# Third layer of a fused four-layer kernel: state scan and feed-forward in one phase instead of two, with a written-out order of their TensorE products

## The reference

```python
h = _layernorm(hidden_states, ln_w, ln_b)
z, x, Bm, Cm, dt = jnp.split(h @ in_proj_w.T, ...)       # widths 512, 128, 128, 512, 8
dt = softplus(dt + dt_bias); A = -exp(A_log)
# 8 heads of 64, state 64, 2 key groups:
#   state = state * exp(dt*A) + dt * x (outer) B ;  y = state . C
y = scan(x, dt, A, B, C) + Dp * x
yf = y * silu(z)
yf = yf * rsqrt(mean(yf * yf) + EPS) * norm_w
mlp = gelu(h @ fc1_w.T + fc1_b) @ fc2_w.T + fc2_b        # inner width 1024
return yf @ out_proj_w.T + mlp + residual
```

## Time and profile before

| | |
|---|---|
| median of 3 runs | 4635.87 us (4613.26 to 4637.77) |
| profiled execution | 4619.02 us, span 4617.3 us |
| third layer from the start of the scan phase to its last add | 1816.1 to 2315.4 us of the span |
| granted TensorE clock, mean of the span | 0.911 of 2.4 GHz |

### The profile page before, as it was taken

The page is one execution under the profiler, slowest core; times in us unless marked ns, Lnnn a source line. Parts: engine busy times, 40 slices in busy tenths (PEclk is TensorE's granted clock), DMA queues, the critical chain, the costliest instruction groups (busy, mean ns, idle before and its releaser), DMA issues. The chain is left out here.

```text
span 4617.3 us, 104974 instructions
## 1 busy us (share of the span) xinstructions
PE 3973.5 (86%) x45271; PEld 2429.6 (53%) x45330; DVE 2323.8 (50%) x4264; ACT 1675.7 (36%) x2628; POOL 1225.8 (27%) x1755
## 2 busy tenths in 40 slices
PE   7887759999975885877989958999999999999869
PEld 3333645555533653444745635666666666656636
DVE  5663244445553134244033245776767676766641
ACT  2345122121121111323111034666556655665532
POOL 2000110000014033131000015555545554555512
PEclk9999669999986986888989978999999999999979
DMA  1000000000012331000010000000000000000000
GB/s 49 1 1 1 29 25 1 11 11 1 11 48 77 122 112 44 0 0 23 0 56 0 0 14 7 10 9 9 9 9 9 11 11 10 9 9 9 7 15 19
DMA packets 38110, 92.10 MB, mean 20 GB/s; under 512 B 7136, under 2 KB 27267, under 8 KB 34142
## 3 DMA queue, kind: packets, MB, share of 16 engines
q1 hardware_dynamic: 27294, 69.66, 4.5%
q0 software_dynamic: 6144, 11.62, 0.9%
q10 hardware_dynamic: 4224, 4.19, 0.3%
HBM read 70.18 MB, written 20.45 MB: 20 GB/s over the span
## 5 line engine op out<-in xcount | busy, mean ns | idle before, releaser
L2622 PE MATMUL ps<-h_normT,h_w 128*128 128x512 f32 (+1 forms) x1008 | 423.6, 525 | 28.5 <-DVE h_xx L3209 20.9
L3143 DVE SCALAR_TENSOR_TENSOR h_cv<-h_raw,h_cw,h_cv 128x1023 f32<-128x1023 f32 (+2 forms) x288 | 391.0, 1367 | 20.2 <-ACT h_cv L2970 19.1
L3287 DVE SCALAR_TENSOR_TENSOR h_st<-h_st,d_gcs,ps 128x64 f32<-128x64 f32 x448 | 123.4, 275 | 341.2 <-PE ps L2918 340.9
L2969 ACT ACTIVATE h_raw<-ps 128x512 f32<-128x512 f32 x192 | 114.1, 594 | 399.1 <-PE ps L2622 398.4
L2622 PEld LDWEIGHTS ps<-h_normT,h_w 128*128 128x128 f32 x1008 | 164.7, 189 | 133.8 <-issue 116.6
L956 PE MATMUL ps<-a_probT,a_v 128*128 128x512 f32 x512 | 227.8, 604 | 0.9 <-DVE a_probT L1094 0.9
L472 ACT ACTIVATE a_prob<-ps 128x1024 f32<-128x1024 f32 (+1 forms) x192 | 154.4, 810 | 194.2 <-PE ps L384 104.3
L2519 POOL TENSOR_TENSOR h_gm<-h_gm,h_tmp 128x15 f32<-128x15 f32 (+7 forms) x480 | 214.9, 448 | 37.6
L2084 PE MATMUL ps<-h_normT,e_wgu 128*128 128x512 f32 (+1 forms) x448 | 204.3, 599 | 6.2 <-DMA e_wd<-in_e_wd 5.0
L1243 POOL MEMSET r_zero<- 128x2048 f32 x1 | 1.8, 1805 | 727.8 <-POOLq L54 727.8
L2918 PEld LDWEIGHTS ps<-h_st,h_mT 64*64 64x64 f32 x1792 | 90.5, 133 | 198.3 <-issue 194.2
(11 more groups left out here) (540 smaller groups left out, 9359.5 us busy)
## 6 DMA issues: line engine op xcount, KB each, us to landing
m_wgu<-in_m_wgu SPq DMA_DIRECT2D x8, 1408.0 KB
h_w<-in_d_w SPq DMA_DIRECT2D x48, 128.0 KB
m_wd<-in_m_wd SPq DMA_DIRECT2D x8, 704.0 KB
m_rows_in<-r_zero SPq DMA_DIRECT2D x4, 1024.0 KB
e_xe<-m_rows_in SPq DMA_DIRECT2D x8, 512.0 KB
m_rows_out<-e_y ACTq DMA_DIRECT2D x8, 512.0 KB
e_wgu<-in_e_wgu SPq DMA_DIRECT2D x1, 3520.0 KB
a_t_raw<-in_t_w SPq DMA_DIRECT2D x4, 768.0 KB
```

Of the source, the lines that this page charges most:

```text
L2622: last = pe.matmul(ps[:, PROJ[m], lo:hi], w[:, kind, k, :], hT[:, k, b * S + tb * BANK + lo:b * S + tb * BANK + hi], start=(k == 0), stop= ...
L3143: dve.scalar_tensor_tensor(out=d, in0=raw[:, kind, 0:S - back], scalar=tap(pr, kind, TAPS3 - 1 - back), in1=d, op0=ALU.mult, op1=ALU.add). ...
```

## The change

`scan2` and `mlp2` become one phase, `scan_mlp2`. All weights are loaded at its start. What it does to the work:

- The token products lose their one-row product; VectorE adds the `dt` bias as it evicts. The decay sums are put between the 10th and the 11th of the 20 B and C products.
- The decay and C-B products are done half by half (`seg(n, g)`, `cb(n, g)`), each half in one bank, and one round ahead of the tile that uses them. The exponential and the multiplication are halved too.
- Two banks form a ring that the inner-layer products (`up`), the gate (`z`) and the turning of y (`turn`) use by a fixed list (`entries`). An entry waits until the entry two before it has been evicted.
- The inner layer is formed for one tile of each sequence at a time (256 columns), two of its four quarters in each round. Its products, and those with `out_proj` and `fc2` (`outputs`), stand between the products of the scan.
- The scaling by the root moves behind the `out_proj` product: VectorE multiplies the product with it as it adds to the residual; `norm_w` is multiplied into `out_proj` once. The mean square and its root are taken tile by tile. GpSimd adds the `fc2` bias to the residual.

The diff, cut to its core:

```diff
 def mixer2(core):
 
 
-    nc = core.nc
-    with Phase(core, "s2") as outer:
-        y = outer.sb("y", [P, NT, DI2])
-        affine_norm2(core)
-        scan2(core, y)
-        mlp2(core, y)
+    affine_norm2(core)
+    scan_mlp2(core)
...
+        SEG, CB, RING, INTRA, INTER, UPD, OUT = 0, 1, (2, 3), 4, 5, 6, 7
...
+        entries = [("up", 0, q) for q in range(4)] + [("z", 0)]
+        for i in range(NT + 1):
+            if i >= 1:
+                entries.append(("turn", i - 1))
+            if i // 2 + 1 < NB:
+                entries += [("up", i // 2 + 1, 2 * (i % 2) + q) for q in range(2)]
+            if i + 1 < NT:
+                entries.append(("z", i + 1))
+        slot = {e: i for i, e in enumerate(entries)}
+        bank = lambda *e: RING[slot[e] % 2]
...
+            sp.dma_start(b2[:], dram["s2_b2"].broadcast_to([P, H])).then_inc(load_mlp, 16)
+            for dst, name in ((f1, "s2_f1"), (b1, "s2_b1"), (op, "s2_op"), (nw, "s2_nw"), (f2, "s2_f2")):
+                sp.dma_start(dst[:], dram[name]).then_inc(load_mlp, 16)
...
+            pool.wait_ge(load_mlp, 16 * 6)
+            for t in range(NT):
+                last = pool.tensor_tensor(core.x[:, t, :], core.x[:, t, :], b2[:], ALU.add)
+            last.then_inc(biased, 1)
...
-                pe.matmul(ps[:, t % 4, 0:TOKW2], core.ones[0:1, :], dtb[0:1, :], start=False, stop=True).then_inc(tokp, 1)
...
+            def room(*e):
+                if slot[e] >= 2:
+                    pe.wait_ge(evicted, slot[e] - 1)
+
+            def seg(n, g):
                 pe.wait_ge(seg_in, n + 1)
-                if n >= 1:
-                    pe.wait_ge(dec_e, n)
-                for g in range(KV2):
-                    pe.matmul(ps[:, g, :], after[:], dseg[:, s, g * J2:(g + 1) * J2, :].rearrange("p h t -> p (h t)"),
-                              start=True, stop=False)
-                    last = pe.matmul(ps[:, g, :], identb[:], notyet[:].rearrange("p h t -> p (h t)"), start=False, stop=True)
-                last.then_inc(segp, 1)
-                if n >= 1:
-                    pe.wait_ge(m_r, n)
-                for g in range(KV2):
-                    last = pe.matmul(ps[:, 2 + g, :], bT[:, g, cols], cT[:, :, cols], start=True, stop=True)
-                last.then_inc(cbp, 1)
-                if n >= 1:
-                    pe.wait_ge(z_r, n)
+                if 2 * n + g >= 1:
+                    pe.wait_ge(dec_e, 2 * n + g)
+                pe.matmul(ps[:, SEG, :], after[:], dseg[:, n % 2, grp(n, g), :].rearrange("p h t -> p (h t)"), start=True, stop=False)
+                pe.matmul(ps[:, SEG, :], identb[:], notyet[:].rearrange("p h t -> p (h t)"), start=False, stop=True).then_inc(segp, 1)
...
+            def up(j, q):
+                room("up", j, q)
+                for i in range(2):
+                    m = 2 * q + i
+                    for k in range(KC):
+                        moving = hT[:, k, :].rearrange("p (b t) -> p b t", b=B)[:, :, j * P:(j + 1) * P]
+                        last = pe.matmul(ps[:, bank("up", j, q), i * B * P:(i + 1) * B * P], f1[:, k, m * P:(m + 1) * P], moving,
+                                         start=(k == 0), stop=(k == KC - 1))
+                last.then_inc(ring_p, 1)
...
+            def outputs(i):
+
+                if i >= 2:
+                    pe.wait_ge(x_added, i - 1)
+                if 0 <= i - 2 < NT:
+                    n = i - 2
+                    pe.wait_ge(evicted, slot["turn", n] + 1)
+                    for c in range(IC2):
+                        last = pe.matmul(ps[:, OUT, H:2 * H], yT[:, n % 3, c * P:(c + 1) * P], op[:, c, :], start=(c == 0), stop=(c == IC2 - 1))
+                if 0 <= i - 1 < NT:
+                    n = i - 1
+                    pe.wait_ge(evicted, slot["up", n // 2, 3] + 1)
+                    for m in range(MC2):
+                        last = pe.matmul(ps[:, OUT, 0:H], hid[:, n // 2 % 2, m, n % 2 * P:(n % 2 + 1) * P], f2[:, m, :],
+                                         start=(m == 0), stop=(m == MC2 - 1))
+                last.then_inc(out_p, 1)
...
+            pe.wait_ge(load_tok, 16 * 2)
             for t in range(NT):
-                if t >= 4:
-                    pe.wait_ge(copied, t - 3)
-                pe.wait_ge(nrm, t + 1)
-                for c in range(IC2):
-                    last = pe.transpose(ps[:, t % 4, c * P:(c + 1) * P], y[:, t, c * P:(c + 1) * P], core.ident[:])
-                last.then_inc(turned, 1)
+                token_projection(t)
+            pe.wait_ge(load, 16 * 4)
+            for n in range(NBC):
+                if n == MID:
+                    decay_sums()
+                turned_projection(n)
+
+            pe.wait_ge(g_r, 3)
+            seg(0, 0)
+            pe.wait_ge(load_mlp, 16 * 6)
+            pe.wait_ge(op_r, 1)
+            up(0, 0)
+            pe.wait_ge(bc_r, NBC)
+            cb(0, 0)
+            up(0, 1)
+            seg(0, 1)
+            up(0, 2)
+            cb(0, 1)
+            up(0, 3)
+            z(0)
+            for i in range(NT + 2):
+                if i >= 1:
+                    outputs(i)
+                if i + 1 < NT:
+                    seg(i + 1, 0)
+                if i < NT:
+                    from_state(i)
+                    to_state(i)
+                if i + 1 < NT:
+                    cb(i + 1, 0)
+                if 1 <= i <= NT:
+                    turn(i - 1)
+                if i < NT:
+                    within(i)
+                if i + 1 < NT:
+                    seg(i + 1, 1)
+                if i // 2 + 1 < NB:
+                    up(i // 2 + 1, 2 * (i % 2))
+                if i + 1 < NT:
+                    cb(i + 1, 1)
+                if i // 2 + 1 < NB:
+                    up(i // 2 + 1, 2 * (i % 2) + 1)
+                if i + 1 < NT:
+                    z(i + 1)
...
+            def up_gelu(j, q):
+                act.wait_ge(ring_p, slot["up", j, q] + 1)
+                if j >= 2:
+                    act.wait_ge(out_p, 2 * j - 2)
+                for i in range(2):
+                    m = 2 * q + i
+                    last = act.activation(hid[:, j % 2, m, :], ps[:, bank("up", j, q), i * B * P:(i + 1) * B * P], ACT.Gelu_apprx_tanh,
+                                          bias=b1[:, m:m + 1])
+                last.then_inc(evicted, 1)
...
+            z_silu(0)
+            for i in range(NT + 1):
+                if i + 1 < NT:
+                    seg_exp(i + 1, 0)
+                if i >= 1:
+                    turn_copy(i - 1)
+                    square(i - 1)
+                if i + 1 < NT:
+                    seg_exp(i + 1, 1)
+                if i // 2 + 1 < NB:
+                    for q in range(2):
+                        up_gelu(i // 2 + 1, 2 * (i % 2) + q)
+                if i + 1 < NT:
+                    z_silu(i + 1)
+                if i >= 1:
+                    root(i - 1)
...
+            def residuals(i):
+
+                dve.wait_ge(out_p, i)
+                if 0 <= i - 1 < NT:
+                    t = order[i - 1]
+                    last = dve.tensor_tensor(core.x[:, t, :], ps[:, OUT, 0:H], core.x[:, t, :], ALU.add)
+                    own.link(last) if i == NT else None
+                if 0 <= i - 2 < NT:
+                    n, t = i - 2, order[i - 2]
+                    dve.wait_ge(sd_r, n + 1)
+                    own.link(dve.reciprocal(rstd[:, n:n + 1], std[:, n:n + 1]))
+                    last = dve.scalar_tensor_tensor(out=core.x[:, t, :], in0=ps[:, OUT, H:2 * H], scalar=rstd[:, n:n + 1],
+                                                    in1=core.x[:, t, :], op0=ALU.mult, op1=ALU.add)
+                last.then_inc(x_added, 1)
...
+            for i in range(NT + 2):
+                if i >= 1:
+                    residuals(i)
+                if i < NT:
+                    n, t, s, b = i, order[i], i % 2, order[i] // NQ
+                    dve.wait_ge(interp, n + 1)
...
+                if i + 1 < NT:
+                    weigh(i + 1, 0)
+                if i < NT:
+                    dve.wait_ge(xp_r, n + 1)
+                    dve.wait_ge(inter_r, n + 1)
+                    own.link(dve.tensor_tensor(inter[:, s, :], inter[:, s, :], xdp[:, s, :], ALU.add))
+                    dve.wait_ge(intra, n + 1)
+                    if n >= 2:
+                        dve.wait_ge(ring_p, slot["turn", n - 2] + 1)
+                        dve.wait_ge(ss_r, n - 1)
+                    dve.tensor_tensor(y[:, s, :], ps[:, INTRA, :], inter[:, s, :], ALU.add).then_inc(y_r, 1)
+                    dve.wait_ge(y_r, n + 1)
+                    dve.wait_ge(evicted, slot["z", n] + 1)
+                    dve.tensor_tensor(y[:, s, :], y[:, s, :], gate[:, s, :], ALU.mult).then_inc(y2_r, 1)
+                if i + 1 < NT:
+                    weigh(i + 1, 1)
+                if i + 2 < NT:
+                    segments(i + 2)
```

(46 more changed lines are left out.)

303 lines of the change are left out of this document (113 added, 190 removed).

## The result

The changed kernel takes 4478.98 us (median of 4 runs, 4477.72 to 4479.81), the kernel before in the same comparison 4626.06 us (4 runs, 4613.26 to 4637.77). The ratio is 0.9682, 95% interval 0.9649 to 0.9715. The forecast was 4484, its range 4455 to 4530. The profiled execution took 4479.81 us, with a mean clock of 0.921.

The account below looks back on a forecast made before the run. No engine was full: TensorE and VectorE took turns in the scan, losing by waits and a falling clock. 110.7 + 33.7 + 6.6 - 3 - 4.5 - 0.5 = 143 us off 4619.0 gave 4476, placed at 4484, range 4455 to 4530.

Parts of the forecast that it names:

- The loop: Scan with third layer's feed-forward: 16 rounds of 18.28 us, bound by TensorE, 292.5 instead of 403.2 us, 110.7 gained.
- handing over: Between engines in the scan rounds: two handovers a round cost something even where nothing is late, 3 us in all.
- the end: Last tile: last turning, its copy, mean square and root, last `out_proj`, two VectorE operations, not covered by other work, 4.5 us.
- fill the scan's waits: Scan rounds: TensorE keeps all its products, and those of the feed-forward occupy its waits; part of the 110.7 us gain.
- A round is 15.9 us: Scan of the kernel before: length of one round read from the profile, with TensorE and VectorE taking turns.
- Token products: Start of the phase: without one-row products the clock rises after about two tiles, 51.7 to 18 us, 33.7 gained.
- Rival A: Token products: the clock stays at 1.2 GHz, 15 us less gain, 4491 to 4508 us; chance 0.22.
- B and C, decay sums: B and C products with three sums within: 41.55 to 34.95 us, 6.6 gained; four banks cover copies starting 0.5 us later.
- Start: Start of the phase: first token weights may come later because of the other weights loaded beside them; 0.5 us allowed.
- Margins: Waits within a round: `z` has at least 0.8 us, second C-B half 2.3, second decay half 4.
- Rival C: Loop: TensorE runs at 1.2 GHz with short products in a row, 260 us more, 4736 us; chance 0.04.
- The forecast's 8 us above the sum: Total: 4476 from the terms raised to 4484 for a median, halfway between the profiled execution and the 17 us higher median.

Follow-up runs that it names:

- the bias product of 128 rows: Changed kernel with a third token product a tile for the bias, 128 rows (127 of them zero), VectorE no longer adding it: 4443.48 us, ratio 0.9676.

## Why the prediction was right

Its total is 5 us off. Its terms, against the profiles:

- **The loop.** Predicted 403.2 to 292.5 with 3 for handing over and 4.5 for the end, 300.0; measured 291.7 (1876.0 to 2167.7). A round was 18.11 us, not 18.28 to 18.6. The 3 us for handing over were wrong: where the operand is there early, one product follows the next without loss, and of the 16 rounds only the last has a wait. That the loop would be bound by TensorE holds: no copy on ScalarE within the margin costs time, and each product taken away does give its own time.
- **Its explanation was wrong in one point.** The prediction said that the products of the feed-forward fill the scan's waits. Without them the scan is just as dense. The sum came out right because at the end only TensorE's own work counts, whichever part removes the waits; that the order would do so without the feed-forward was not foreseen. Of the 111.5 us of the loop, 90 are the scan's own: its loop was 236.9 us, and without the feed-forward it is 181.3, less 27.5 for 16 `out_proj` products and 6.9 for turning, about 147. That is 16 times the 9.15 us of products at full clock, so all of the waiting and all of the slow clock are gone. By the earlier trace rows the waits were 61.1 us (236.85 - 175.75) and the lower clock 29.3 (175.75 - 146.4). What is left, about 21, is the way between the phases and its cold start. These are worked out, not measured apart. The look-ahead has no part in them.
- **A reading that was off.** "A round is 15.9 us" holds for every second round; those between took 14.8. The sum did not use it.
- **Token products.** Predicted 51.7 to 18; measured 16.9, and 15.7 where the bias alone was changed. The reason holds: it was the one-row products that kept the clock low. Rival A did not come.
- **B and C, decay sums.** Predicted 41.55 to 34.95; measured 36.4. What is missing is mostly one wait of 1.10 us for ScalarE's copy (`c_bT` L1921) behind a late `dA_r`. The prediction saw that wait coming and thought the four banks would cover it. But the softplus on VectorE, which comes ahead of `dA_r`, was slow beside GpSimd's adds (last section). The adds, "under the B and C products", were priced at nothing because TensorE covers them; VectorE, which does not, is what they cost. Moved behind `dA_r`, the stretch is 35.0. It is 35.0 too with the bias product of 128 rows, where the adds stay where they are but the softplus comes later: they end at 1803.50, and only the first of its operations (1802.87, 0.71 us) is still slow.
- **Start.** Predicted +0.5; measured +1.4 (2.9 to 4.3 us from the first weight transfer to the first product).
- **Margins.** `z` predicted 0.8, measured 1.36; the gelus of 256 columns take 0.42 each (0.84 for two), 0.45 was assumed. The drain that the Trainium skill, ScalarE: Activation LUTs, section What ACT_TABLE_LOAD costs, puts at about 1380 ns for each switch does not show in this trace: four switches a round have their activation 1.30 us after the load starts, and the loop has no wait for it.
- **The clock with short products.** It stayed at 1.00 through 288 us. Rival C did not come. The turning products are 0.43 of 18.11 us (1998.58 to the next at 1999.01). The Trainium skill, TensorE: Matmul & The Clock Gate, section Part 4: PE-mode transpose, says that they do not count as busy for the clock; no run here shows it: at this share the clock stayed at 1.00. Nor did the clock fall with gaps of 0.88 and 1.64 us in each round.
- **Outside the change.** The third layer's terms sum to 150.0 us, and the span lost 139.2. The rest is 2.3 us more before the third layer and 8.5 us more in the last layer, from the first of its heads' products to the last of its output products: 1651.8 us before, 1660.3 after. In the profiles of the other kernels, none of which changes that stage, it varies from 1643.2 to 1684.5 us. Between before and after the busy time of VectorE, ScalarE and GpSimd in that stage differs by at most 1.7 us; that of TensorE is 5.9 us longer (1555.7 and 1561.6), at a mean clock of 0.95 instead of 0.96. Why it is so stays open. The forecast's 8 us above the sum, put there for the median, made up for part of it by luck: the sum itself was 7 us short of the gain of the third layer.

## What to carry to other kernels

A stretch with waits on all engines is priced by the work of the engine that fills up once the waits are gone; but to know which edit removes them, take each away alone: here the work that was said to fill the gaps filled none. And compare what you take away with the kernel before: the look-ahead is worth 22 us, but both kernels have it. Where one engine waits for another at the same place in each round, look at what stands between the two on the waiting engine: products that are ready, put there, end the wait. Write out the margins of a round and spend work on them knowingly: up to the margin it is free, beyond it it counts in every round. Look for products of one row in a stretch at clock 0.50: a bias that another engine adds while it evicts gave 36 us here, where its 16 products would have taken 7 at full clock (0.44 each by the run with 128 rows).

## What was not expected of the hardware

VectorE and GpSimd slow each other. The same multiplication of 128x1024 on VectorE (the segments) and the same multiplication of 128x512 on GpSimd, side by side in the kernel without look-ahead and feed-forward, from the timelines of both engines:

```profile
1930.14 2.06 DVE L1992 TENSOR_TENSOR c_dseg<-c_upto,c_dA 128x1024 f32<-128x1024 f32 x1
...
1931.09 2.02 POOL L1742 TENSOR_TENSOR c_xdp<-c_tok,c_dp 128x512 f32<-128x512 f32 x1
```

and in the changed kernel, where they fall apart in time:

```profile
2005.34 1.22 DVE L2016 TENSOR_TENSOR c_dseg<-c_upto,c_dA 128x1024 f32<-128x1024 f32 x1
...
2003.29 1.04 POOL L1744 TENSOR_TENSOR c_xdp<-c_tok,c_dp 128x512 f32<-128x512 f32 x1
```

2.06 against 1.22 us, and 2.02 against 1.04. The kernel before had the slow form in each round, on the path; what part of the gain this is was not measured apart (at 0.84 us a round at most 13 us, an estimate). The softplus shows the same. In the changed kernel, beside GpSimd's bias adds:

```profile
1835.86 11.14 POOL L1728 TENSOR_TENSOR x_resid<-x_resid,c_b 128x256 f32<-128x256 f32 x16 [10.79 <-DMA c_f<-in_s_f]
...
1840.82 0.65 DVE L2047 TENSOR_SCALAR c_egc<-c_dA 128x128 f32<-128x128 f32 x1
```

and with the adds moved behind it:

```profile
1829.01 0.23 DVE L2049 TENSOR_SCALAR c_egc<-c_dA 128x128 f32<-128x128 f32 x1
```

0.65 us against 0.23.
